# The experts' residual added through ScalarE and a turned-back product instead of a folded matrix

## What is computed

```python
def _moe(x, Wg, W1, b1, W2, b2):            # x = y
    idx = jnp.argmax(xf @ Wg.T, axis=-1)
    for e in range(E):
        m = (idx == e)[:, None]
        h = jax.nn.relu(xf @ W1[e] + b1[e])
        out = out + m * (h @ W2[e] + b2[e])
y = _layer_norm(x + _mha(...), g1, be1)
z = _layer_norm(y + _moe(y, Wg, W1, b1, W2, b2), g2, be2)
```

## Time and profile before

| | |
|---|---|
| median of 3 runs | 650.33 us |
| the profiled execution, its own time | 650.18 us |
| its span in the profile | 648.2 us |
| TensorE busy (PE) | 597.2 us, 92% |
| VectorE busy (DVE) | 442.9 us, 68% |
| ScalarE busy (ACT) | 387.5 us, 60% |
| GpSimd busy (POOL) | 393.0 us, 61% |
| first application of the experts, from the first turned tile | 236.87 us |
| second application, from the first turned tile | 550.18 us |

### The profile page before, as it was taken

One profiled execution on the slowest core, in us unless ns is written; L12 is line 12 of the kernel. 1 busy time (PEld: TensorE's weight loads), 2 busy tenths in 40 slices (PEclk: granted clock), 3 DMA queues, 4 the chain that ended last, 5 costly groups with the idle time before them and its releaser, 6 DMA issues.

```text
span 648.2 us, 18632 instructions
## 1 busy us (share of the span) xinstructions
PE 597.2 (92%) x5750; PEld 517.4 (80%) x5750; DVE 442.9 (68%) x2139; ACT 387.5 (60%) x973; POOL 393.0 (61%) x636
## 2 busy tenths in 40 slices
PE   6999999986999889999979999999779988999993
PEld 4889999854777668999966788787568876999993
DVE  2676778875588978988841434434348886798984
ACT  3587778977888445666423454654378862555661
POOL 4465688994177765888851334334205777477886
PEclk9999999989999999999998999999799998999998
DMA  5970000121244483333150000000013445333320
GB/s 134 314 265 10 2 18 19 41 98 31 55 123 133 128 249 94 99 94 89 48 142 2 18 17 17 25 19 17 25 39 100 132 134 134 88 91 90 89 80 24
DMA packets 58478, 53.89 MB, mean 83 GB/s; under 512 B 8236, under 2 KB 52693, under 8 KB 58061
## 3 DMA queue, kind: packets, MB, share of 16 engines
q1 hardware_dynamic: 51434, 36.19, 20.4%
q0 software_dynamic: 5568, 12.96, 5.8%
q10 hardware_dynamic: 1378, 3.55, 1.5%
HBM read 31.33 MB, written 19.83 MB: 79 GB/s over the span
## 4 chain that ended last, share of the span: by engine, by line
PE 65%; DVE 12%; ACT 7%; issue 6%; POOL 5%; DMA 2%; ACTq 1%; DVEq 0%; POOLq 0%; SPq 0%
PE bank L1630 9%; PE wide L1641 6%; PE wide L1818 5%; PE wide L1791 5%; PE bank L1804 4%; PE wide L668 4%; PE bank L1641 3%; POOL rstd L1522 3%; PE wide L498 2%; PE wide L712 2%; PE bank L721 2%; PE wide L685 2%; PE wide L157 2%; ACT rows_e L1363 2%; PE wide L1643 1%
## 5 line engine op out<-in xcount | busy, mean ns | idle before, releaser
L1630 PE MATMUL bank<-zt,late 128*128 128x128 f32 x624 | 85.7, 279 | 2.3 <-DVE room_f L1692 2.1
L1630 PEld LDWEIGHTS bank<-zt,late 128*128 128x128 f32 x624 | 77.4, 193 | 4.3 <-DVE room_f L1692 3.6
L1531 POOL DMA_INDIRECT sorted_dram<-rows_e,pos x64 | 64.1, 1002 | 26.7 <-issue 26.7
L1571 POOL TENSOR_TENSOR rstd<-var_e,half_neg 128x1 f32<-128x1 f32 x78 | 61.8, 792 | 18.0 <-DVE var_e L1701 15.9
L1653 ACT ACTIVATE late<-we 128x512 f32 x80 | 50.4, 630 | 22.8 <-PE bank L1630 19.0
L1522 POOL TENSOR_TENSOR rstd<-var_m,half_neg 128x2 f32<-128x2 f32 x32 | 23.2, 724 | 57.2 <-DVE nmean L1437 57.0
L1641 PE MATMUL wide<-late,room_f 128*128 128x128 f32 x416 | 55.1, 275 | 0.0
L1766 POOL TENSOR_TENSOR var_m<-mvs,eps 128x4 f32<-128x4 f32 (+1 forms) x20 | 4.0, 198 | 81.7 <-DVE mvs L1892 81.7
L1641 PEld LDWEIGHTS wide<-late,room_f 128*128 128x128 f32 x416 | 50.6, 192 | 0.1
L1363 ACT ACTIVATE rows_e<-rows_w,shift,rstd 128x128 f32<-128x128 f32 x64 | 28.1, 487 | 32.1 <-POOL shift L1524 32.1
L1578 POOL DMA_INDIRECT out<-xout,dest x39 | 40.3, 1034 | 11.0 <-issue 10.8
(11 more groups left out here) (316 smaller groups left out, 1793.0 us busy)
## 6 DMA issues: line engine op xcount, KB each, us to landing
rows_e<-sorted_dram SPq DMA_DIRECT2D x78, 128.5 KB, 2.1
we<-L_ffn_W SPq DMA_DIRECT2D x16, 256.0 KB
early<-late SPq DMA_DIRECT2D x128, 32.0 KB
rows_e<-y_dram SPq DMA_DIRECT2D x32, 128.0 KB, 2.7
sorted_dram<-L_attn_a_x ACTq DMA_DIRECT2D x2, 1028.0 KB
y_dram<-grams SPq DMA_DIRECT2D x16, 128.0 KB, 1.8
y_dram<-att_t SPq DMA_DIRECT2D x16, 128.0 KB, 1.8
xa<-x_dram SPq DMA_DIRECT2D x3, 640.0 KB, 6.5
```

Of the source, the lines that this page charges most:

```text
L1531: nc.gpsimd.indirect_dma_start(sorted_dram[n][:, :], bass.IndirectOffsetOnAxis(ap=pos[:, p % 3, t:t + 1], axis=0), pay[:, p % PAYS, t, :], ...
L1571: nc.gpsimd.tensor_tensor(rstd[:, s % 3, 0:1], var_e[:, s % 3, :], half_neg[:, 0:1], ALU.pow).then_inc(g["rstd"], 1)
L1630: last = nc.tensor.matmul(to[:, (m % 2) * P:(m % 2 + 1) * P], we_t[:, c1, m * P:(m + 1) * P], zt[:, c1, 0, 0:P], start=True, stop=True)
```

## The change

The residual is no longer a product with a folded matrix. ScalarE reads the turned tile in TB a second time, multiplies it by g1 and adds be1 + b2[e], both one number per feature, which in the turned layout is one per partition. The result goes to the second half of `zt`. TensorE adds it to the sums of W2 by a product with the identity in transposing mode, which turns it back. `be2c` holds be1 + b2[e] as one column per expert: eight loads of one column each and one addition of VectorE replace a load of all b2 to all partitions and the hats 15 and 16. VectorE's copy per tile is 512 columns instead of 640. The turn of tile i + 1 now waits for both copies of tile i.

```diff
-EW = F + F + D
+EW = F + F
...
+        be2c = sb("be2c", [P, E])
...
-        bias_b2, row_f, row_a = parts(rows_f, (E * D,), (4 * D,), (3 * D,))
+        row_f, row_a = parts(rows_f, (4 * D,), (3 * D,))
...
-                   (bias_b2[:, :], f["b2"].rearrange("(a e) n -> a (e n)", a=1).to_broadcast([P, E * D])),
                    (g2f[:, :], row(f["g2"]).to_broadcast([P, D]))]
+        loads_o += [(be2c[:, e:e + 1], column(f["b2"][e])) for e in range(E)]
...
-        hats_f += [hat(4 * D, fold_f[:, :], ident4, None, we[:, e:e + 4, 2 * F:], rows=bias_b2[:, e * D:(e + 4) * D])
-                   for e in (0, 4)]
...
-        HATS_LATE = {PAIRS + 1: (11, 13), PAIRS + 2: (13, 14), PAIRS + 3: (14, 15), PAIRS + 4: (15, 16), PAIRS + 5: (16, 17),
-                     PAIRS + 6: (17, 18)}
+        HATS_LATE = {PAIRS + 1: (11, 13), PAIRS + 2: (13, 14), PAIRS + 3: (14, 15), PAIRS + 4: (15, 16)}
...
+            nc.vector.tensor_scalar(be2c[:, :], be2c[:, :], col[:, 3:4], None, ALU.add).then_inc(fold_step, 1)
             hat_copies(dve, hats_f[HATS_FIRST:HATS_RAMP], N_A + HATS_FIRST, of_vector=True)
...
# TensorE, experts
-                        after(pe, g["zt"], o + i)
+                        after(pe, g["zt"], 2 * (o + i))
                         nc.tensor.transpose(TB[:, 0:P], zs(s % ZS)[:, 0:D], ident[:, :]).then_inc(g["turned"], 1)
                     if has(1):
-                        pe.wait_ge(g["zt"], o + i)
+                        pe.wait_ge(g["zt"], 2 * (o + i) - 1)
...
-                        nc.tensor.matmul(VB[c2][:, 0:P], zt[:, c2, 0, 0:P], we_t[:, c2, 2 * F:], start=False,
-                                         stop=True).then_inc(g["v"], 1)
+                        pe.wait_ge(g["zt"], 2 * (o + i - 1))
+                        nc.tensor.matmul(VB[c2][:, 0:P], zt[:, c2, 0, P:2 * P], ident[:, :], start=False, stop=True,
+                                         is_transpose=True).then_inc(g["v"], 1)
...
# ScalarE, experts
                     e = act.value_load(owner[0:1, bass.ds(i, 1)], min_val=0, max_val=E - 1)
...
+                    held.append(e)
...
                     if has(0):
+                        nc.scalar.activation(zt[:, c, 0, P:2 * P], TB[:, 0:P], ACT.Identity, scale=col[:, 2:3],
+                                             bias=be2c[:, bass.ds(held[i], 1)]).then_inc(g["zt"], 1)
                         after(act, g["hid_b"], o + i - 1)
```

More of the change, by code:

```diff
@@ L1044, in build @@
         HATS_RAMP = 11
-        HATS_LATE = {PAIRS + 1: (11, 13), PAIRS + 2: (13, 14), PAIRS + 3: (14, 15), PAIRS + 4: (15, 16), PAIRS + 5: (16, 17),
-                     PAIRS + 6: (17, 18)}
-        assert len(hats_f) == HATS_LATE[PAIRS + 6][1]
+        HATS_LATE = {PAIRS + 1: (11, 13), PAIRS + 2: (13, 14), PAIRS + 3: (14, 15), PAIRS + 4: (15, 16)}
+        assert len(hats_f) == HATS_LATE[PAIRS + 4][1]
         @on("vector")
@@ L1508, in _ @@
                 nc.vector.tensor_copy(gone[:, 2, 1, :], rooms_row[:, :]).then_inc(fold_step, 1)
-                dve.wait_ge(fold_step, 6 + 3 * n)
+                dve.wait_ge(fold_step, 7 + 3 * n)
                 pipeline(dve, PAIRS, 14, 1, body, PAIRS)
@@ L1649, in _ @@
                 g = e_s
+                held = []
                 def first_matrix(i, c):
@@ L1672, in _ @@
                     act.wait_ge(hat_kept, N_F)
+                    act.wait_ge(fold_step, 5)
                 first_matrix(0, 0)
@@ L1904, in _ @@
                 nc.vector.tensor_scalar_mul(bo[:, :], bo[:, :], ROW).then_inc(fold_step, 1)
-                dve.wait_ge(fold_step, 7)
+                dve.wait_ge(fold_step, 8)
                 pipeline(dve, PAIRS, 5, 3, body, FIRST)
```

## The result

The changed kernel takes 645.06 us (median of 15 runs, 639.56 to 649.24) against 650.33 for the kernel before (15 runs, 644.12 to 652.26). The ratio is 0.9919, with a 95% interval of 0.9895 to 0.9944: 0.8% faster, 5.3 us, where 7.5 were forecast. The profiled execution took 646.23 us, its span 644.3 against 648.2.

The account below looks back on a forecast made before the run. TensorE was taken to bound the steady expert tiles, 2.12 us falling to about 2.01. Terms -6.9 + 0.1 - 0.7 - 1.3 + 1.3 = -7.5 us from 650.18 gave 642.7, stated as 642.8 us; range 640.8 to 646.6.

Parts of the forecast that it names:

- The fifth product: On TensorE per tile: a transposing product of 0.11 us replaces one of 0.22; 62 times on the chain, -6.9 us.
- the four products ahead of the lists: Fifth products before VectorE makes the lists, 2 per application, counted among the 62 that each save 0.1115 us.
- ScalarE: One added activation per tile makes its step 1.80 us, below TensorE's 2.01: no steady cost, +0.1 in the first tiles.
- the slower rival: ScalarE paces the tile: register-address stops at the new activation make its step 2.28 us, the kernel 659.5; chance 0.04.
- GpSimd: In steady tiles its own 1.94 us step keeps up with 2.01; as rival it paces, 644.3 or 649.3 us, chance 0.10.
- the hold: GpSimd's reciprocal root held by VectorE's 640-column copy, 0.87 against 0.69 us; must shrink by 0.11 to keep up.
- VectorE's copy: Per-tile copy falls from 640 to 512 columns, 0.063 us each; 11 copies on the chain, -0.7 us (0 to -1.1).
- The hats: End of the first routing: removing two hat copies of 0.59 and 0.68 us from VectorE's chain gives -1.3 us.
- The clock: Without the hats TensorE's granted clock falls in the first routing as in the second; +1.3 us, bounds 0 and 1.7.
- The price of 1.66 us: Kernel before, last count to tile 10's turn: 24.75 us in the second application against 23.09 in the first.

Follow-up runs that it names:

- e3: The kernel before with only the fifth product changed to a transposing product with the identity; 644.09 us, ratio 0.9927 to before.
- e7: The changed kernel with ScalarE's new activation done twice per tile, the first result unread; 646.94 us, ratio 0.9968 to before.
- e1: The changed kernel with the spin ahead of the first routing's last counts lengthened from one product to three; 640.68 us, ratio 0.9892 to before.
- e2: The changed kernel with hats 15 and 16 and their load kept, their result unread; 642.9 us, ratio 0.9912 to before.

## Why the prediction was right, and where its sizes were off

**The fifth product**: right in kind and size per tile (0.11 for 0.22). The count was too high: the four products ahead of the lists gave nothing, though they stood on the chain (e3). The chain itself has 64 rows of L1643, 30 in each steady part, where the prediction read 62 and 29; 60 x 0.1115 us are 6.7.

**ScalarE**: right; 1.80 us per step was a ceiling. What could have held the tile up was the place that the prediction named, the turn that waits for the new activation: e7 puts the pace of that loop at 2.07 less 0.34, 1.73 us. The stop of 0.24 us at the register load, on which the slower rival rested, even shrank: from the end of the new activation (291.76) to the W1 copy are 0.14 us.

**GpSimd**: right that it keeps up, with more room than the 0.07 us of the forecast. The 0.69 us from which the hold was read was itself held; with no copy near, the root takes 0.58, in the kernel before too:

```profile
324.42 0.58 POOL L1571 TENSOR_TENSOR rstd<-var_e,half_neg 128x1 f32<-128x1 f32 x1
```

So the hold was 0.29 us before and is 0.18 now. In both kernels the root ends 0.43 us after VectorE's copy does (291.67 and 291.24 before, 291.54 and 291.10 after). The Trainium skill's rule of an exclusive lock ("SBUF — State Buffer", "Who interferes with whom") fits that in the steady part. But it did not fix the period: in e3 the copy has its old 640 columns and the tile still takes 2.00 us, with a root of 0.75. GpSimd comes as early as it can and is held until the copy is done. What was not forecast is in the second application, which gained 2.5 us where 3.2 were due. Once per execution GpSimd stands still for 2.4 us between a reciprocal root and a scatter:

```profile
585.71 1.03 POOL L1577 DMA_INDIRECT out<-xout,dest  x1 [2.44 <-issue]
...
587.39 0.35 DVE L1715 SCALAR_TENSOR_TENSOR xout<-rows_w,rstd,rows_e 128x128 f32<-128x128 f32 x1 [1.34 <-POOL rstd L1570]
...
588.99 0.71 PE L1629 MATMUL bank<-zt,late 128*128 128x128 f32 x4 [0.47 <-DVE room_f L1698]
```

The kernel before has the same stop, of 2.37 us; VectorE waited 0.92 for it, and TensorE's next products were at most 0.14 us longer than usual. At 2.0 us per tile there is less slack to take it up: 1.34 on VectorE and 0.47 on TensorE, and the tile there takes 2.74 us instead of 2.00. What causes the stop is open; nothing was tried on it.

**VectorE's copy**: 0.071 us per copy by the groups' means (0.424 for 0.495), 0.063 forecast. The ramp from tile 0 to tile 10 is 20.79 us in e1 against 21.80 before. Half of that 1.0 is there with the hats kept (21.29 in e2), about what the shorter copies give; the other half goes with the hats.

**The hats**: right in size, -1.3 forecast, 1.5 by e1 against e2, but in other places: 1.0 in the counts, where both copies' 1.27 us were expected, and 0.5 in the ramp, which was not priced. That the whole stretch came to the forecast's -1.9 without the clock is partly luck, since this 0.5 stands in for 0.3 of the hats and 0.2 of the products that were not there.

**The clock** is the step whose size failed: it was put at +1.3 us, with bounds 0 and 1.7. The fall came where it was foreseen, but it cost 3.3 us, outside the bounds. The price of 1.66 us was read from the second application of the kernel before, and the forecast went below it, because "a fall should come earlier and be over sooner". It came earlier and was not over sooner: 232.3 to 242.5, 10.2 us, where the one behind the price lasted from 546.9 to 553.7, 6.8 us. Of the 3.3 us, 0.4 lie between the first and the last of the four counts (9.52 us against 9.13 in e1) and 2.9 behind them (24.83 against 21.93). About 0.7 of these is the last count held back by the spins (0.77 us from VectorE's addition to the count, 0.06 in e1): they were taken as filling a gap, and at half the clock they are longer than the gap. With 3.3 the forecast would have been 644.8, and with the second application's 0.6 us 645.4; measured were 645.06. That it comes so close is partly luck: the profiled execution that these terms are read from took 646.23.

The 1.1 us that the changed kernel loses between the applications go with the longer fall at 338 us, in a part that the change does not touch. The cause of its length is open.

## What to carry to other kernels

Where work leaves an engine's gaps, price what the gaps become: here two products off the critical path, 1.8 us of TensorE's work, kept the clock up, and their removal cost more than the work they stood beside. Fill such gaps with idle products up to just below the length of the gap at full clock, and check in the trace that the next count does not wait for them. Trading a product for an activation pays when the product is on the busiest engine and the activation fits in the other's idle time per tile; doing the activation twice tells how much room is left, here 0.27 us.

## What was not expected of the hardware

- A product in transposing mode adds to a group of ordinary float32 products in PSUM, as one instruction of 0.11 us beside their two of 0.11.
- At half the clock, three spin products of 128 x 256 that fill 1.3 us (six instructions 0.215 apart in e1) take 2.7 and delay what is behind them, so the cure against a fall deepens one that has happened.
- GpSimd stands still once per execution for 2.3 to 2.4 us in the second application, in each of the nine profiles (2.29 to 2.44 us).
- The same program's first 225 us differed by up to 2 us between executions (225.85 and 227.94 at the first mark of the changed kernel), and the fall of the clock at the start of the second attention block, which all nine profiles have, lasts from 3.4 to 10.2 us. A difference of one profile against another should be cut at marks before any of it is put down to an edit.
